# Turning the attention probabilities as two row pieces, 0-63 and 64-111, in the array mode of the scores, with the waits on a one-column product

## The reference

```python
# x: (32, 112, 256), context: (32, 375, 256), h: 16 heads
q, k, v = x @ Wq, context @ Wk, context @ Wv        # split in heads
sim = jnp.einsum('bihd,bjhd->bhij', q, k) * SCALE   # 112 x 375 for each head
attn = jax.nn.softmax(sim, axis=-1)
out = jnp.einsum('bhij,bjhd->bihd', attn, v)
```

## Time and profile before

| | us |
|---|---|
| median of 3 runs | 2522.17 |
| lowest and highest | 2519.28, 2523.46 |
| the profiled execution, whole | 2521.23 |
| its span, first to last instruction | 2519.4 |
| TensorE products busy | 2398.6 (95% of the span) |
| VectorE, ScalarE, GpSimd busy | 1701.0, 1590.8, 1592.4 |

### The profile page before, as it was taken

How to read it: one execution, slowest core, us unless ns; L and a number is a source line. 1 busy time by engine, 2 the same in 40 slices (tenths; PEclk the granted TensorE clock), 3 DMA queues, 4 the chain that set the end, 5 groups by cost and what they waited for, 6 DMA issues and landing times.

```text
span 2519.4 us, 59698 instructions
## 1 busy us (share of the span) xinstructions
PE 2398.6 (95%) x18926; PEld 1791.1 (71%) x18926; DVE 1701.0 (68%) x4475; ACT 1590.8 (63%) x4337; POOL 1592.4 (63%) x1846
## 2 busy tenths in 40 slices
PE   7999999999999999999999999999999999998576
PEld 5777777777777777777777777777777777775335
DVE  6666666676666666766666677666666766666674
ACT  4666666766666667666666666666666666665444
POOL 2666676666667766666677666666766666676405
PEclk9999999999999999999999999999999999999799
DMA  4100000000000000000000000000000000001002
GB/s 147 34 10 10 10 8 10 2 10 10 10 10 10 8 7 5 10 10 10 10 10 8 4 8 10 10 10 10 8 10 2 10 10 10 10 2 44 19 0 58
DMA packets 34519, 36.95 MB, mean 15 GB/s; under 512 B 2804, under 2 KB 32964, under 8 KB 34500
## 3 DMA queue, kind: packets, MB, share of 16 engines
q1 hardware_dynamic: 34500, 36.71, 4.9%
HBM read 29.36 MB, written 7.34 MB: 15 GB/s over the span
## 4 chain that ended last, share of the span: by engine, by line
PE 74%; DVE 9%; issue 6%; ACT 6%; POOL 4%; DMA 0%; ACTq 0%; DVEq 0%; SPq 0%; POOLq 0%
PE ps L326 16%; PE pt L405 16%; PE ps L395 14%; PE pa L417 7%; PE pa L452 5%; PE ps L379 4%; DVE z L1121 4%; PE pa L432 4%; POOL prob L1388 2%; ACT prob L748 2%; POOL qrs L1431 1%; DVE nmx L975 1%; PE pt L549 1%; PE ps L445 1%; ACT z L801 1%
## 5 line engine op out<-in xcount | busy, mean ns | idle before, releaser
L975 DVE TENSOR_REDUCE nmx<-ps 112x2 f32<-112x750 f32 x512 | 480.0, 938 | 198.6 <-PE ps L395 198.5
L1388 POOL TENSOR_TENSOR prob<-prob,rinv 112x375 f32<-112x375 f32 x512 | 404.0, 811 | 225.9 <-DVE rinv L991 219.8
L1388 POOL TENSOR_TENSOR f1w_room<-f1w_room,rinv 112x375 f32<-112x375 f32 x512 | 404.8, 815 | 61.7 <-DVE rinv L991 53.1
L709 ACT ACTIVATE room<-ps 128x375 f32<-128x375 f32 (+2 forms) x480 | 227.6, 487 | 290.6 <-PE ps L326 290.6
L966 DVE COPY probT<-pt 125x336 f32<-125x336 f32 x512 | 254.0, 496 | 116.5 <-PE pt L405 116.4
L709 ACT ACTIVATE probT<-pt 125x336 f32<-125x336 f32 x512 | 231.1, 451 | 120.1 <-PE pt L405 117.1
L405 PEld LDWEIGHTS pt<-ident,prob 112*125 112x125 f32 x1536 | 190.6, 189 | 128.8 <-issue 68.7
L405 PEld LDWEIGHTS pt<-ident,f1w_room 112*125 112x125 f32 x1536 | 197.4, 188 | 118.6 <-issue 51.9
L1411 POOL TENSOR_TENSOR krs<-krs,nhalf 125x48 f32<-125x48 f32 x32 | 257.0, 8030 | 0.0
L395 PE MATMUL ps<-kT,q 64*112 64x375 f32 x1024 | 229.6, 526 | 18.9 <-ACT f1w_room L748 16.6
L405 PE MATMUL pt<-ident,f1w_room 112*125 112x112 f32 x1536 | 238.5, 287 | 2.0 <-POOL f1w_room L1388 0.7
(11 more groups left out here) (248 smaller groups left out, 5136.5 us busy)
## 6 DMA issues: line engine op xcount, KB each, us to landing
ctok<-in_ctx SPq DMA_DIRECT2D x32, 375.0 KB
xin<-in_x SPq DMA_DIRECT2D x32, 112.0 KB, 2.0
x_rows<-x SPq DMA_DIRECT2D x32, 112.0 KB, 1.9
out<-probT SPq DMA_DIRECT2D x8, 448.0 KB, 3.2
room<-x_rows SPq DMA_DIRECT2D x1, 2576.0 KB, 13.7
stage<-in_f1w SPq DMA_DIRECT2D x2, 1024.0 KB, 5.4
stage<-in_wk SPq DMA_DIRECT2D x1, 1024.0 KB, 8.9
stage<-in_wv SPq DMA_DIRECT2D x1, 1024.0 KB, 11.3
```

The lines of the kernel that those rows point to most:

```text
L709: return act.activation(dst, src, ACT.Copy)
L975: top = dve.tensor_reduce(nmx[:, g:g + 2], ps[0:T, 2 * (i % 2):2 * (i % 2) + 2, 0:S], AX_X, ALU.max, negate=True)
L1388: pool.tensor_tensor(prob(i, n), prob(i, n), rinv[:, g:g + 1].to_broadcast([T, S]), ALU.mult).then_inc(s["normed"], 1)
```

## The change

The six transposes of a turn become twelve. Each 112-row piece is cut into rows 0-63 and rows 64-111, and the two pieces lie on the two row halves of the array, as the two heads of the scores do. All pieces of rows 0-63, of both heads, go to bank 0 of `pt` (6 x 64 columns), all of rows 64-111 to bank 1 (6 x 48 columns). ScalarE's copy therefore takes 125 x 384 and VectorE's 125 x 288. All waits of the turn, for both copies of the pair before and for the normalisation of both heads, now stand at its start, on a new bfloat16 product of 64 rows by 128 columns with one moving column, whose result nobody reads. `pT` is raised by one twice as before, but only once each bank is complete, so by the last two transposes.

```diff
+        ROWS = ((0, 64), (64, T))
...
             def turn(i, part, b):
 
+                if part != OPENING or i >= 1:
+                    pe.wait_ge(s["pT_even"], at(i, part, b))
+                    pe.wait_ge(s["pT_odd"], at(i, part, b))
+                pe.wait_ge(s["normed"], 2 * at(i, part, b) + 2)
+                pe.matmul(pt[:, 0, 511:512], identb[0:64, :], identb[0:64, 0:1], start=True, stop=True)
                 for n in range(2):
-                    pe.wait_ge(s["normed"], 2 * at(i, part, b) + n + 1)
-                    if part != OPENING or i >= 1:
-                        pe.wait_ge(s["pT_odd" if n else "pT_even"], at(i, part, b))
                     for t in range(KT):
-                        last = pe.transpose(pt[0:SK, n, t * T:(t + 1) * T],
-                                            prob(i, n)[:, t * SK:(t + 1) * SK], ident[0:T, 0:T])
-                    last.then_inc(s["pT"], 1)
+                        for bank, (r, e) in enumerate(ROWS):
+                            col = (n * KT + t) * (e - r)
+                            last = pe.transpose(pt[0:SK, bank, col:col + e - r],
+                                                prob(i, n)[r:e, t * SK:(t + 1) * SK], ident[r:e, r:e])
+                            if n == 1 and t == KT - 1:
+                                last.then_inc(s["pT"], 1)
...
-                copy(probT[:, 2 * (i % 4), :, :], pt[0:SK, 0, 0:KT * T].rearrange("p (k t) -> p k t", k=KT))\
-                    .then_inc(s["pT_even"], 1)
+                copy(probT[:, 2 * (i % 4):2 * (i % 4) + 2, :, 0:64],
+                     pt[0:SK, 0, 0:2 * KT * 64].rearrange("p (n k t) -> p n k t", n=2, k=KT)).then_inc(s["pT_even"], 1)
...
-                dve.tensor_copy(probT[:, 2 * (i % 4) + 1, :, :],
-                                pt[0:SK, 1, 0:KT * T].rearrange("p (k t) -> p k t", k=KT))\
+                dve.tensor_copy(probT[:, 2 * (i % 4):2 * (i % 4) + 2, :, 64:T],
+                                pt[0:SK, 1, 0:2 * KT * (T - 64)].rearrange("p (n k t) -> p n k t", n=2, k=KT))\
                     .then_inc(s["pT_odd"], 1)
```

## The result

| | before | after |
|---|---|---|
| median of the runs, us | 2522.82 | 2586.91 |
| lowest and highest, us | 2519.28, 2523.63 | 2585.8, 2589.09 |
| ratio, 95% interval | | 1.0257 [1.0241, 1.0273] |
| the profiled execution, whole, us | 2521.23 | 2589.09 |
| median of the 31 distances from pass to pass, us | 72.35 | 74.17 |

The change costs 64 us. The forecast said 2568, 46 more than before, with a range up to 2595. The sign and the range held; 18 us are missing from the sum. Most of this part is about them.

A forecast was written before the change was run, and what follows sets the result against it. TensorE was taken to bound the kernel, with mode gains ending in the wait on VectorE's copy. Terms summed to +1.45 us a pass, +45 over 31 passes, +1.5 for opening and closing: 2568 us, range 2545 to 2595.

The forecast's parts named there:

- Modes: Scores and turns share one array mode: turn to scores saves 0.19 us, scores to turn 0.09.
- Rival (c): Scores and turns still differ in mode: block 1's two-step period 4.05 us rather than 3.99, total 2574 us; chance 0.10.
- (d): A turn's row pieces load one after the other, 0.65 us more a turn, total 2800 us; chance 0.05.
- (b): A 64-row piece loads in half the time, 0.055 us, a turn taking 0.33 less, total 2474 us; chance 0.06.
- (e): Gain and loss cancel, leaving the time within 0.2% of before; chance 0.07.
- The gain is lost in the wait: Block 1's even turns could begin 0.37 us earlier, but VectorE's copy, behind row_max, comes no sooner.
- Rival (a): The array sets the pace, copies never late: 0.41 us saved each two-step period, total 2476 us; chance 0.07.
- turn 2: Turn 2 starts only when GpSimd's normalisation is done, values at 978.89 against 978.55: +0.34 us a pass.
- turns 4 and 6 together: Block 3: all transposes wait for VectorE's copy, values at 983.59 against 983.29: +0.30 us each, +0.60 a pass.
- turns 8, 10 and 12 together: Block 1: load behind the copy at 994.60 against 994.64, turn 0.85 for 0.84: -0.03 us each, -0.09 a pass.
- the end: End of pass: turn 13 +0.05 us, projections behind it +0.15, turns 14 and 15 +0.20 each; together +0.60.
- That is 0.11 from the copy's end to the load: Delay from the end of VectorE's copy to a turn's load, 0.11 us, used for turns in blocks 3 and 1.

The follow-up runs named there:

- Experiment 4: The changed kernel with row pieces only in odd turns up to 11, even turns and last three in the old form: 2496.95 us, ratio 0.9906 to the kernel before.
- experiment 2: The changed kernel with the wait on the normalisation first and the waits on the two copies last: 2570.61 us, ratio 1.0181 to the kernel before.

## Why the prediction was right in its sign and short in its size

**Modes: right.** Scores and turns run into each other, twelve transposes load as fast as six, and turns 14 and 15 and the projections behind turn 13 pay 0.17 to 0.18 for a change that they did not have. Rival (c) would show a gap at 1014.54 and (d) loads of over 0.8. (b) would have halved the 0.74. All three are out, and (e) is out by the time itself.

**The gain is lost in the wait: right, and it decided the sign.** Row_max starts 0.94 behind the scores, the copy behind that, and the turn behind the copy, whatever the array could do. Rival (a) is out for this kernel. Experiment 4 shows that it was not far: with the wait at the half, 0.72 a pass came through.

**The terms.** In us a pass, forecast and measured: turn 2 +0.34 and +0.29; turns 4 and 6 together +0.60 and +0.75; turns 8, 10 and 12 together -0.09 and +0.13; the end +0.60 and +0.65, of which 0.15 shows up only at the start of the next pass, and together with turn 2 makes up the first row of the table (0.29 + 0.15). The sum is +1.45 and +1.82. That the end comes out so near is luck in part: up to the values behind turn 14 it is 0.32 for a forecast 0.40, behind turn 15 0.18 for 0.20, and the 0.15 at the next pass's start was not forecast.

**The step that failed** is "That is 0.11 from the copy's end to the load", carried into "copy ends ..., load at ..." of the turns of both blocks. I took it from a wait that was the last thing before its transposes. In the new form it is 0.24 to 0.25, for the arithmetic for the value of the wait on `normed` stands between (experiment 2). That is +0.13 on each of five turns. Two small terms work the other way: from the small product's load to the next group are 0.81 and not 0.85, since the small product seems to cost about 0.01 where I took 0.05, and the copy takes 0.43 to 0.44 and not 0.45. Net, 0.07 to 0.08 on each of five turns, 0.37 a pass, 11 us in all. At turn 2, where GpSimd is late and `normed` the last wait anyway, the load follows within 0.05 (997.27 + 1.58 = 998.85, load at 998.90), as the forecast took it from the earlier trace rows. The order of the waits should have been checked there: which wait is late, and what stands behind it.

**The rest**, 64 - 46 - 11 = 7 us, is the clock. The forecast had given it no term. By the means over the executions, 0.986 and 0.981, the changed kernel spends about 2 x 0.005 x 2587 = 26 us more at the lower level. In the slow pass about 7 us at it cost 2.5, so an estimate of the price is 26 x 2.5 / 7 = 9 us. The kernel with the old closing gives another: 10 us between its runs at 0.989 and those at 0.981 and 0.982, so some 7 us for 0.005. Both are near the 7. Why it falls more often is not shown.

**The bounds.** The term that missed had none. For the small product and the copy both ends were given, but the latency stood as a single number from two rows, and it was multiplied by five turns and 31 passes. With an upper end of 0.25 the sum would have run to 2590 and the range beyond 2600. That the measured time lies within the range is luck in part: the width came from the small product and the copy, which moved the time the other way, and not from the two terms that were missing.

## What to carry over

When several half-way waits are gathered in front of a block, the block starts with the latest of them: look, before, at how far ahead of its last input the first half used to run, since that lead is the price. A gain on an engine that waits for another at the next station is worth only what the wait leaves; put the new form where the engine isn't waited on (here the odd turns), keep the old one where it is. Put the wait that ends last at the end, directly ahead of its instruction, and those that need arithmetic first.

## What the runs showed of the hardware

- A change of the array's mode costs 0.17 to 0.19 us each way here (projections 1.59 for 1.41, turn 0.81 for 0.64), and transposes of row pieces follow products of the same tiling without one (loads at 1014.54 right behind the scores').
- Two fp32 pieces of 64 and 48 rows, one on each row half, load in the time of one piece of 112 rows: 12 in 0.74, 6 in 0.73.
- From the end of VectorE's copy to TensorE's load pass 0.11 to 0.12 us when the sequencer's wait for it is the last thing ahead of the load, and 0.24 to 0.25 when register arithmetic for a further wait stands between them.
- Four more products of one column cost 0.025 us each. The load of a single one starts 0.01 ahead of the next loads.
- The granted clock fell to its lower level for some 7 us in 9 of the 155 passes of five profiled executions (four kernels), always at the same place of the pass, at 2.5 us each. It came back at different times after the same idle stretch in the closing. The times of one kernel go with the mean clock: 2576.2 at 0.989 and 2585.4 to 2587.3 at 0.981 and 0.982, 2605.6 to 2607.7 at 0.987 and 0.988 and 2620.1 at 0.978.
